# The attention stage rewritten: transposed scores, with the weighted sum of group c - 2 ahead of the scores of group c in every slot

## The reference, cut to what matters

```python
h = jnp.maximum(_layernorm(x, axis=-1), 0.0)
agg = jnp.einsum('vn,bvd->bnd', U, h)
h1 = jax.nn.relu(agg @ W1 + b1)              # (b, 120, 128)
out = h1 @ W2 + b2                           # (b, 120, 1024)
g_x = _maxpool2(_pw_conv(out, g_w, g_b)).transpose(0, 2, 1)      # (b, 512, 128)
theta_x = _pw_conv(out, th_w, th_b).transpose(0, 2, 1)           # (b, 1024, 128)
phi_x = _maxpool2(_pw_conv(out, ph_w, ph_b))                     # (b, 128, 512)
f = jnp.einsum('blc,bcm->blm', theta_x, phi_x)                   # (b, 1024, 512)
y = jnp.einsum('blm,bmc->blc', jax.nn.softmax(f, axis=-1), g_x).transpose(0, 2, 1)
w_y = _pw_conv(y, wo_w, wo_b)                # then batch norm with fixed statistics
z = w_y + out
return x + jnp.einsum('nv,bvd->bnd', U, z) + z
```

## Time and profile before

| | |
|---|---|
| time, median of 3 runs | 3787.45 us (3784.44 to 3789.18) |
| the profiled execution's own time | 3789.16 us |
| its span, first to last instruction | 3786.5 us |
| PE busy | 3460.0 us (91%) |
| DVE busy | 3246.9 us (86%) |
| ACT busy | 2320.0 us (61%) |
| POOL busy | 1972.5 us (52%) |
| slices of the attention stage (from 947 us on) | PE 90% or more in each, clock at full speed |
| mean granted clock of TensorE | 0.967 of full speed |

### The profile page before, as it was taken

One profiled execution on the slowest core, in us unless ns is written; L12 is line 12 of the kernel. 1 busy time (PEld: TensorE's weight loads), 2 busy tenths in 40 slices (PEclk: granted clock), 3 DMA queues, 4 the chain that ended last, 5 costly groups with the idle time before them and its releaser, 6 DMA issues.

```text
span 3786.5 us, 77925 instructions
## 1 busy us (share of the span) xinstructions
PE 3460.0 (91%) x19037; PEld 2769.1 (73%) x19037; DVE 3246.9 (86%) x8804; ACT 2320.0 (61%) x4998; POOL 1972.5 (52%) x2194
## 2 busy tenths in 40 slices
PE   7999995006999999999999999999999999999999
PEld 5777775005887888878888788878888788887887
DVE  6888883997888888888888888888888888888888
ACT  6999997003556565565555555655565555656555
POOL 2333331003666666665666656666566665666655
PEclk9999998557999999999999999999999999999999
DMA  4444443000111111111111111111111111111111
GB/s 119 102 103 103 104 104 78 0 0 11 42 42 44 49 42 42 42 45 49 42 42 42 46 47 42 42 42 47 47 42 42 42 47 47 42 42 42 47 47 42
DMA packets 55558, 192.52 MB, mean 51 GB/s; under 512 B 7547, under 2 KB 8820, under 8 KB 55532
## 3 DMA queue, kind: packets, MB, share of 16 engines
q1 hardware_dynamic: 55532, 192.25, 19.7%
HBM read 129.32 MB, written 62.91 MB: 51 GB/s over the span
## 4 chain that ended last, share of the span: by engine, by line
PE 49%; DVE 23%; ACT 13%; issue 13%; DVEq 1%; ACTq 1%; POOL 0%; SPq 0%; DMA 0%; POOLq 0%
PE ps_P L698 6%; PE ps_O L630 6%; PE ps_M L630 5%; PE ps_M L632 5%; PE ps_O L632 5%; PE ps_M L631 5%; PE ps_O L631 5%; DVE pT_lo L1207 5%; DVE nmx L1196 4%; ACT junkx L435 4%; PE ps_S L630 3%; PE ps_S L632 3%; PE ps_S L631 3%; ACT frelu L444 3%; PE ps_M L674 3%
## 5 line engine op out<-in xcount | busy, mean ns | idle before, releaser
L403 POOL TENSOR_TENSOR pn<-p,ri 128x512 f32<-128x512 f32 x1024 | 1130.6, 1104 | 1120.3 <-DVE ri L1201 1120.3
L521 ACT ACTIVATE p<-ps_S,nmx 128x512 f32<-128x512 f32 x1024 | 705.0, 688 | 764.6 <-DVE nmx L1196 764.4
L1196 DVE TENSOR_REDUCE nmx<-ps_S 128x1 f32<-128x512 f32 x1024 | 700.4, 684 | 70.1 <-PE ps_S L632 58.4
L1207 DVE TENSOR_TENSOR pT_lo<-ps_P,pT_hi 128x512 fp32r<-128x512 f32 x1024 | 690.4, 674 | 3.0 <-ACT pT_hi L529 3.0
L529 ACT ACTIVATE pT_hi<-ps_P 128x512 fp32r<-128x512 f32 x1024 | 607.1, 593 | 41.0 <-PE ps_P L698 22.3
L698 PE MATMUL ps_P<-ident,pn 128*128 128x128 f32 x4096 | 618.1, 273 | 1.8 <-POOL pn L403 1.8
L698 PEld LDWEIGHTS ps_P<-ident,pn 128*128 128x128 f32 x4096 | 492.0, 141 | 123.1 <-POOL pn L403 35.6
L630 PE MATMUL ps_S<-ph_hi,th_hi 128*128 128x512 f32 x1024 | 488.3, 477 | 3.3 <-DVE ph_lo L1171 3.3
L630 PE MATMUL ps_O<-pT_hi,v_hi 128*120 128x512 f32 x1024 | 411.9, 402 | 28.5 <-DVE pT_lo L1207 28.3
L632 PE MATMUL ps_S<-ph_lo,th_hi 128*128 128x512 f32 x1024 | 405.5, 396 | 0.0
L632 PE MATMUL ps_O<-pT_lo,v_hi 128*120 128x512 f32 x1024 | 404.2, 395 | 0.0
(11 more groups left out here) (310 smaller groups left out, 6729.7 us busy)
## 6 DMA issues: line engine op xcount, KB each, us to landing
xin<-in_x_dram SPq DMA_DIRECT2D x128, 480.0 KB, 4.2
xt<-in_x_dram SPq DMA_DIRECT2D x128, 480.0 KB, 4.2
out_dram<-xt SPq DMA_DIRECT2D x128, 480.0 KB, 3.3
W1s<-in_L_gnn_W_dram SPq DMA_DIRECT2D x1, 512.0 KB, 3.8
W2f<-in_L_gnn_W_dram SPq DMA_DIRECT2D x1, 512.0 KB, 4.7
cth<-in_L_gnn_b_dram SPq DMA_DIRECT2D x1, 512.0 KB, 4.1
cph<-in_L_gnn_b_dram SPq DMA_DIRECT2D x1, 512.0 KB, 6.6
cg<-in_L_gnn_b_dram SPq DMA_DIRECT2D x1, 512.0 KB, 8.1
```

Source lines behind the costliest of these rows:

```text
L403: pool.tensor_tensor(pn[:, c % 4, :], p[:, c % 2, :], ri[:, c % 4:c % 4 + 1].to_broadcast([128, M]), ALU.mult).then_inc(pn_sb, 1)
L521: act.activation(p[:, c % 2, :], ps_S[c % 2][:, :], ACT.Exp, bias=nmx[:, c % 4:c % 4 + 1], accum_out=rs[:, c % 4:c % 4 + 1]).then_inc(p_sb, 1)
L1196: dve.tensor_reduce(nmx[:, c % 4:c % 4 + 1], ps_S[c % 2][:, :], AX.X, ALU.max, negate=True).then_inc(max_sb, 1)
L1207: T(pT_lo[:, half, :, l], ps_P[c % 2][:, :].rearrange("p (m l) -> p m l", l=128), pT_hi[:, half, :, l].bitcast(F32), ALU.subtract).then_in ...
```

## The change

All of the attention stage is rewritten; the engines' lists still have eight slots a turn.

- The projections are no longer made from `T`. PE forms `out` itself, bias included (`o0`, `o1`: hT_hi/hT_lo times W2, three instructions for each half of 512 columns), ACT and DVE split it into `o_hi`, `o_lo`. The bias row of `out` is row N (120), a row of ones is row 121 and, in `o_hi` only, row 122 (`NA`) carries the negative maxima. `ph`, `g` and `res` are products of `Chi`, `Clo` with `o_hi`, `o_lo`. The constants `cth`, `cph`, `cg`, `cres` go.
- theta is not formed. `Q` = theta's weights times phi (three instructions), so that scores are out^T Q.
- Row maxima come from coarse scores: `c0` to `c7`, one instruction each (`o_hi` times `Q_hi`), a DVE maximum for each, two PE transposes of the maxima (`m0`, `m1`, 128x4 to 4x128), an ACT copy into `mrow`, and a DMA of that row into row 122 of `o_hi` (`put_max`).
- Exact scores come transposed (128 of the 512 phi columns on the partitions, 512 of the 1024 columns along the free axis), the maximum already subtracted by row 122. ACT takes exp (`expo`, no bias, no sum), copies the leading part (`lead`, `p_hi`), POOL subtracts (`spill`, `p_lo`), and PE forms the weighted sum (`attend`) two slots later. No transposes, no `pn`.
- `v` has a leading column of ones, so row 0 of the weighted sum is the row of denominators. ACT copies the sum to `y` (`O0`, `O1`). SP moves `y[0]` to 128 partitions (`dcol`), DVE inverts (`inv`), SP writes it to DRAM and reads it back broadcast to 121 partitions (`rbc`), DVE multiplies (`norm`), POOL adds `acc` = residual + x (`finish`), SP stores.
- In the LayerNorm stage `b_mean` is folded into `b_sum`. In the setup some memsets, a reduction of the weights and a split of `th_w` are new, and the work on the four constants goes.

PE's slot, and the lists:

```diff
+            def scores(b, par, c):
+                j, m = c // 4, c % 4
+                if m == 0:
+                    pe.wait_ge(mrow_in[j], b * 16 + 16)
+                if c == 0:
+                    pe.wait_ge(Qlo_sb, b + 1)
+                late(pe, p_sb, b * CH + c - 1)
+                k = slice(m * 128, (m + 1) * 128)
+                f = slice(j * 512, (j + 1) * 512)
+                three(ps_E[c % 2][:, :], Q_hi[0:NM, par, k], Q_lo[0:NM, par, k], o_hi[0:NM, par, f], o_lo[0:NM, par, f],
+                      True, True).then_inc(E_ps, 1)
+
+            def attend(b, par, c):
...
+                pe.wait_ge(phi_sb, b * CH + c + 1)
+                pe.wait_ge(plo_sb, b * CH + c + 1)
+                three(ps_O[j][0:NO, :], v_hi[:, par, m, 0:NO], v_lo[:, par, m, 0:NO], p_hi[:, c % 4, :], p_lo[:, c % 4, :],
+                      m == 0, m == 3).then_inc(O_ps, 1)
+
+            def turn(b, par):
                 for c in range(CH):
-                    if c >= LAG:
-                        turned(b, c - LAG)
-                    elif not first:
-                        turned(b - 1, c - LAG + CH)
-                    scores(b, par, c)
-                    attend_slot(b, par, c, first)
-                    pieces(head, PE_SLOTS[c], b, par, first)
+                    if c >= LAG and runs(b):
+                        attend(b, par, c - LAG)
+                    if c < LAG and runs(b - 1):
+                        attend(b - 1, 1 - par, c - LAG + CH)
+                    if runs(b):
+                        scores(b, par, c)
+                    pieces(head, PE_SLOTS[c], b, par)
...
-LAG = 3
-PE_SLOTS = [[("res1", -1), ("g0", 0), ("h", 1)], [("g1", 0), ("T", 1)], [("th0", 1), ("v", 0)],
-            [("ph0", 1), ("th1", 1)], [("ph1", 1)], [], [("res0", 0)], []]
-ACT_SLOTS = [[("h", 1)], [("T", 1)], [("v", 0), ("th0", 1)], [("th1", 1)], [], [("ph", 1)], [], []]
-DVE_EARLY = [[], [], [], [], [("fin0", -1)], [], [("ph", 1)], [("fin1", -1)]]
-DVE_LATE = [[("g0", 0), ("gm0", 0), ("h", 1)], [("g1", 0), ("T", 1), ("gm1", 0)], [("th0", 1), ("v", 0)],
-            [("ph0", 1), ("th1", 1), ("pm0", 1)], [("ph1", 1), ("pm1", 1)], [], [], []]
+LAG = 2
+PE_SLOTS = [[("v", 0), ("ph0", 1), ("m1", 0)], [("ph1", 1), ("res0", 0)], [("g0", 1)], [("g1", 1), ("Q", 1)],
+            [("c0", 1), ("c1", 1), ("res1", 0)], [("c2", 1), ("c3", 1), ("h", 2)],
+            [("c4", 1), ("m0", 1), ("o0", 2), ("c5", 1)], [("c6", 1), ("c7", 1), ("o1", 2)]]
+ACT_SLOTS = [[("v", 0), ("m1", 0)], [("ph", 1)], [("O1", -1)], [("Q", 1)], [], [("h", 2)],
+             [("m0", 1), ("o0", 2), ("O0", 0)], [("o1", 2)]]
+DVE_SLOTS = [[("v", 0), ("pm0", 1)], [("pm1", 1), ("xr0", 0), ("ph", 1)], [("gm0", 1)], [("gm1", 1), ("inv", -1), ("Q", 1)],
+             [("c0", 1), ("c1", 1), ("xr1", 0)], [("c2", 1), ("c3", 1), ("h", 2), ("norm", -1)],
+             [("c4", 1), ("c5", 1), ("o0", 2)], [("c6", 1), ("c7", 1), ("o1", 2)]]
+POOL_FETCH, POOL_FINISH = 4, 6
+SBANK = [0, 1, 0, 1, 1, 0, 1, 0]
+MBANK = [0, 1]
```

The coarse scores' waits on PE, ACT's order, SP's division and DVE's end of it:

```diff
+                if piece[0] == "c":
+                    c = int(piece[1])
+                    if c < 2:
+                        late(pe, max_sb, b * CH)
+                        late(pe, mrow_sb, b * 2)
+                    elif c == 4:
+                        pe.wait_ge(max_sb, b * CH + 4)
+                    elif c == 5:
+                        pe.wait_ge(mrow_sb, b * 2 + 1)
+                    else:
+                        pe.wait_ge(max_sb, b * CH + c - 1)
...
+                    mm(ps_S[SBANK[c]][:, :], o_hi[0:NA, par, c * 128:(c + 1) * 128], Q_hi[0:NA, par, :],
+                       start=True, stop=True).then_inc(S_ps, 1)
...
+            def turn(b, par):
                 for c in range(CH):
...
+                    if runs(b):
+                        expo(b, c)
+                        lead(b, c)
+                    pieces(head, ACT_SLOTS[c], b, par)
...
+            def invert(b, par):
+                sp.wait_ge(O_sb, b * 2 + 2)
+                late(sp, rcol_sb, b)
+                sp.dma_start(dcol[:, :], y[0:1, par, :]).then_inc(den_in, 16)
+
+                sp.wait_ge(rcol_sb, b + 1)
+                sp.dma_start(r_dram[0:1, :], rcol[:, :]).then_inc(rrow_out, 16)
+                sp.wait_ge(rrow_out, b * 16 + 16)
+                sp.dma_start(rbc[:, :], r_dram[0:1, :].to_broadcast([NO, D])).then_inc(rbc_in, 16)
...
+                if runs(b + 1):
+                    load_x(b + 1, 1 - par)
+                if runs(b):
+                    put_max(b, par, 1)
+                if runs(b - 1):
+                    invert(b - 1, 1 - par)
+                if runs(b + 1):
+                    put_max(b + 1, 1 - par, 0)
+                if runs(b - 1):
+                    store(b - 1, 1 - par)
...
+                if piece == "norm":
+                    dve.wait_ge(rbc_in, b * 16 + 16)
+                    dve.wait_ge(O_sb, b * 2 + 2)
+                    T(y[:, par, :], y[:, par, :], rbc[:, :], ALU.mult).then_inc(norm_sb, 1)
```

More of the change, by code:

```diff
@@ L151, in build @@
             ps_m = [pb(f"ps_m{i}", [128, 512], early) for i in range(2)]
[L154 to L163, removed]
+        pst = sb("pst", [128, 2, H])
+        hT_hi = sb("hT_hi", [H, N], F32R)
+        hT_lo = sb("hT_lo", [H, N], F32R)
         phf = sb("phf", [128, M])
-        ph_hi = sb("ph_hi", [128, 2, M], F32R)
-        ph_lo = sb("ph_lo", [128, 2, M], F32R)
+        ph_hi = sb("ph_hi", [128, M], F32R)
+        ph_lo = sb("ph_lo", [128, M], F32R)
         gf = sb("gf", [128, M])
[L168 to L176, removed]
+        nmx = sb("nmx", [128, CH])
+        mrow = sb("mrow", [4, 2, 128], F32R)
+        p = sb("p", [128, 4, 512])
+        p_hi = sb("p_hi", [128, 4, 512], F32R)
+        p_lo = sb("p_lo", [128, 4, 512], F32R)
+        y = sb("y", [NO, 2, D])
+        acc = sb("acc", [NO, 2, D])
+        dcol = sb("dcol", [128, 8])
+        rcol = sb("rcol", [128, 8])
+        rbc = sb("rbc", [NO, D])
         ps_S = [pb(f"ps_S{i}", [128, 512]) for i in range(2)]
-        ps_P = [pb(f"ps_P{i}", [128, 512]) for i in range(2)]
+        ps_E = [pb(f"ps_E{i}", [128, 512]) for i in range(2)]
         ps_O = [pb(f"ps_O{i}", [128, 512]) for i in range(2)]
@@ L249, in rounds, with pieces, periods, runs @@
                 body(i * 2 + 1, 1)
-        def pieces(head, slot, b, par, first):
+        def pieces(head, slot, b, par):
             for name, of in slot:
-                if of >= 0 or not first:
+                if not isinstance(b, int) or 0 <= b + of < B:
                     head(b + of, (par + of) % 2, name)
+        def periods(eng, turn):
+            for b in range(-2, 2):
+                turn(b, b % 2)
+            rounds(eng, 2, B - 2, turn)
+            for b in range(B - 2, B + 1):
+                turn(b, b % 2)
+        def runs(b):
+            return not isinstance(b, int) or 0 <= b < B
+        def upto(count, most):
+            return min(count, most) if isinstance(count, int) else count
         block = ctx.enter_context(nc.Block())
@@ L321, in _ @@
+            periods(sp, turn)
+            for par in range(2):
+                sp.wait_ge(o_out[par], B * 8)
         @block.gpsimd
@@ L424, in _ @@
-            theta_lo(0, 0, 0)
-            theta_lo(0, 0, 1)
-            turn(0, 0)
-            turn(1, 1)
-            rounds(pool, 2, B, turn)
+                    if runs(b):
+                        spill(b, c)
+                    if c == POOL_FETCH and runs(b + 2):
+                        fetch(b + 2, par)
+                    if c >= POOL_FINISH and runs(b - 1):
+                        finish(b - 1, 1 - par, c - POOL_FINISH)
+            periods(pool, turn)
         @block.scalar
@@ L540, in _ @@
[L540 to L546 removed]
+                    late(act, O_ps, b * CH - CH)
+                    act.activation(v_hi[:, par, :, 1:NO], ps_M[BANK["v"]][:, 0:4 * N].rearrange("p (m n) -> p m n", n=N),
+                                   ACT.Copy).then_inc(vhi_sb, 1)
@@ L549, in _ @@
+            periods(act, turn)
         @block.tensor
```

545 lines of the change are left out of this document (244 added, 301 removed).

## The result

The changed kernel takes 3681.38 us (median of 4 runs, 3680.86 to 3681.97); the kernel before took 3787.74 beside it. The ratio is 0.972 (95% interval 0.9704 to 0.9737): 2.8% or 106 us faster. The forecast was 3729, inside a range of 3665 to 3930; rival 1 had 3678. The profiled execution's span is 3680.1 us.

What follows compares the result with a forecast made beforehand. The division's loop through DMAs was taken to bound the changed kernel at 13.9 + 8.1 = 22.0 us a sample: 3786.5 + 128 x (22.0 - 22.52) + 8 = 3728, plus 2.7, less 1.7: 3729 us, range 3665 to 3930.

Steps and rivals of the forecast that it cites:

- rival 1: Attention period: PE and the wait at c5 bound, landings S at most 7.7; 21.6 us a sample, 3678 us; chance 0.17.
- The forecast case: Attention stage: 21.75 to 22.3 us a sample, 3695 to 3770 us in all; chance 0.44.
- the division sets it: Attention period: the loop through the division's DMAs, 22.0 us, exceeds the 21.6 of PE's path and sets the period.
- The wakes of SP and DVE: Division: SP wakes 0.34 after engines and 0.18 after a landing, two of DVE 0.16 us.
- The small landings: Division: the two 4 KB transfers taken to land in 1.75 and 1.7 us, 1.6 to 2.2 each.
- the floor of 1.6: Division's small transfers: none lands in less than 1.6 us, since all transfers carry that fixed part.
- landings S: Division: sum of its three DMA landings, 8.1 us (7.3 to 9.4), added to 13.9 for the period.
- PE's work: Attention stage: 83 products of 512 columns, v, h, small transposes and FP32 extras, 20.9 us a sample.
- The wait at c5: Slot 5's coarse score waits 0.65 us for ACT's copy of m0 behind exp(6) and p_hi(6), making PE's path 21.6.
- The leading weighted sum costs nothing: PE slots: attend(c - 2) ahead of scores finds p_lo ready 4.35 us after its slot's start, needed at 4.70 or later.
- The cliff: Norm on DVE: past S = 8.34 it stands behind GpSimd's p_lo(6) and the period jumps to 23.5 us.
- Fixed work: Outside the periods: start +2, LayerNorm -3, constants -3, pipeline fill +4, end +8; sum +8 us (0 to +15).

Runs made afterwards that it cites:

- experiment 3: Changed kernel with one more transfer in the division: reciprocals also written to a second DRAM row and awaited before the broadcast; 3892.36 us.
- experiment 6: Changed kernel with ScalarE's copy of the first maxima row (m0) moved ahead of exp(6) and p_hi(6), TensorE's order unchanged; 3607.20 us.
- experiment 4: Experiment 3's kernel, its extra transfer kept, with the reciprocals broadcast over 128 partitions instead of 121; 3694.89 us.
- experiment 5: Changed kernel with the two parts of each TensorE slot swapped, scores first and the weighted sum after them; 3561.99 us.
- experiment 8: Experiment 5's kernel with four unused FP32 128x128 transposes put ahead of each of eight product groups a sample; 4007.82 us.
- experiment 2: Changed kernel with the three products of g0 (slot 2) computed twice, 0.70 us more TensorE work a sample where TensorE does not wait; 3768.64 us.
- experiment 9: Changed kernel with only the broadcast of reciprocals widened from 121 to 128 partitions; 3680.08 us.
- experiment 7: Experiment 5's kernel with the small transposes of maxima (m1) moved directly behind v, ahead of ph0; 3561.67 us.

## Why the prediction was right, and where it was not

The sign, the main mechanism and the range held. The forecast case did not: **the step that failed is "the division sets it"**, the choice between 21.6 and 22.0, and the reason is the size of its terms. Predicted was 13.9 + 8.1 = 22.0; the loop is 11.6 + 9.45 = 21.05 (experiments 3 and 6). Of the 0.95 us between them, 0.2 is the way back (11.8 against 11.6). The other 0.73 is in the division. The wakes of SP and DVE, which I put at 0.68 together after one pair of rows, take about 0.1, since SP issues 0.03 behind ACT or DVE (the wake of 0.17 is not general). The small landings are 2.0 and 1.4 for 1.75 and 1.7, so the floor of 1.6 that I set under every transfer does not hold. The reciprocal is 0.20 for 0.15, and the broadcast 4.5 in the mean for 4.65. It does run on 11 engines, but the 4.2 under it was too long and the three packets more too cheap: 128 rows, with eight on each engine, take 3.7, and 121 rows 0.8 more (experiment 4), not 0.66. (Where the prediction says that equal spreading makes the sum 0.45 lower, it must say unequal.)

With the loop at 21.05 the greater of the two is c5's 21.6, which is rival 1: 3678 forecast, 3681 measured. It was given 0.17. Its number came, but not by its condition: it asked for landings S of at most 7.7, and they are 7.9 (2.0 + 1.4 + 4.5). That the division fell below c5 is owed mostly to the wakes, which no rival varied.

**PE's work**: 20.9 predicted, 20.66 measured where nothing waits (experiment 5). Most of the difference is in the two small transposes, which hold PE for 0.03 each (2511.66 to 2511.69) and not 0.12. The price of the transposes removed was right: 3.5 predicted, 3.49 measured (experiment 8).

**The wait at c5**: 0.65 predicted, 0.63 measured, with its cause (the rows at 2512.80 and 2513.10), and experiments 2 and 6 show that it is on the path: work elsewhere adds to the period (+87 us), and with the wait taken away the time falls by 74 us.

**The leading weighted sum costs nothing**: its own wait does not (3.9 us in all). But the step counted only what attend waits for, not what it delays. It puts the scores, and with them exp(6), 0.7 us later in the slot, and that is what makes c5 wait. The prediction had the wait and the order, and did not set one against the other: with the scores first it is gone, and with it and the wait ahead of h 119 us.

**The cliff**: the mechanism is right and its price near: a period of 23.25 for 23.5, norm 2.06 us in the median (experiment 3), removed by a broadcast 0.78 us shorter (experiment 4). In the changed kernel norm stands ahead of p_lo(6), as I had it, by 1.08 us and not 0.24, mostly because the division is shorter. Missed was the near edge: the GpSimd operation ahead, p_lo(5), holds norm as well (experiment 9). The "GPSIMD Engine Reference" of the Trainium skill (Specifications) says that GpSimd shares SBUF interfaces with VectorE; experiments 3, 4 and 9 agree in both directions.

**Fixed work**: +8 predicted, +10 measured. By the timelines of DVE the start costs 1.3 (predicted 2; `colA` at 17.30, now at 18.58), LayerNorm's end gives back 2.0 (3; `EB` at 641.04, now at 640.37), the constants 2.5 (3; the first `phf` at 878.66, now at 875.47), so some 13 are left for filling the pipeline and the end (12); these were not taken apart.

**Not seen in the changed kernel**: the wait before c6 or c7 on DVE's maxima appears only when the division binds (0.99 in experiment 3, 0.1 in the mean in experiment 6). PE has no named wait on h_lo, v_lo or mrow_in, as predicted.

## What to carry to other kernels

When a part is moved ahead of another on the engine that bounds, price both what it waits for and what it pushes back: here the first was nothing, and the second, every exp 0.7 us later in its slot, cost 3% of the time. When two loops come out within 2% of each other, the sum cannot choose between them, so spread the chances over both. And an operation that excludes another engine's has a window with two edges: find both before paying for a faster transfer.

## What the hardware showed that I had not expected

- A broadcast of one 4 KB row from DRAM over 128 partitions (512 KB, 16 engines) is used by norm 3.7 us behind its issue, over 121 partitions (484 KB, 11 engines) 4.5 (means of experiments 4 and 3). The larger transfer is the faster one.
- A product of two SBUF operands on DVE (1.23 us alone) that becomes ready while GpSimd's p_lo runs, 0.5 to 1.2 us before its end, ends 1.07 to 1.09 us behind it, wherever in it that happens (experiments 3 and 9, 211 samples). Its duration in the profile, 1.6 to 2.3 us, contains the time in which it is kept out.
- A 4 KB write to DRAM lands in 1.4 us, a 4 KB row spread over 128 partitions of SBUF in 2.0.
- SP issues the transfers of the division 0.03 us after the end of the ACT or DVE operation they wait for. The store of the kernel before stood 0.17 behind its operation; what makes the difference is open.
- exp without a bias operand and without the row sum takes 598 ns, where with both it took 688:

```profile
L579 ACT ACTIVATE p<-ps_E 128x512 f32<-128x512 f32 x1024 | 612.5, 598 | 892.9 <-PE ps_E L675 818.4
```

- The 0.08 us that seems lost behind a group of FP32 products goes with the group, and is not saved by putting two groups together (experiment 7).
